# Attention shift and scale of layer 0: from two summed rows broadcast through DRAM to factors that TensorE makes for all 128 partitions

## The chip, the cores and the metric

The kernel runs on one core of a Trainium2 chip. The metric is the device time of one execution in microseconds (us); lower is better. The engines are PE (TensorE, matmuls; PEld is its weight load), DVE (VectorE), ACT (ScalarE), POOL (GpSimd) and SP, which here only issues DMAs. Each engine takes its own list of instructions in order and meets the others through semaphores.

## The reference

Two transformer blocks run one after the other on x of shape (2, 1024, 288), both conditioned on `cond` of shape (2, 288). Cut to what matters here:

```python
ada = silu(cond) @ W_ada + b_ada                  # (2, 6*288)
shift_msa, scale_msa, gate_msa, shift_mlp, scale_mlp, gate_mlp = split(ada, 6)
h = layernorm(x) * (1.0 + scale_msa) + shift_msa  # 288 numbers each for a batch element
x = x + gate_msa * attention(h, W_qkv, b_qkv, W_proj, b_proj)
h = layernorm(x) * (1.0 + scale_mlp) + shift_mlp
x = x + gate_mlp * (gelu(h @ W_fc1 + b_fc1) @ W_fc2 + b_fc2)
```

In layer 0 the attention goes over the 1024 tokens with 16 heads of 18; in layer 1 each token attends over its own heads.

## The kernel before

The 2048 tokens are 16 tiles of 128 tokens (tile t, eight for each of the two batch elements), with the 288 channels along the free dimension of `x_sb`. A modulation row therefore has to stand in all 128 partitions: `ada[:, b, place, :]` holds place 0 to 5 (shift, scale, gate of the attention; shift, scale, gate of the MLP) for batch element b.

At the entry of layer 0 the work is ordered by hand, as each engine's list.

- ACT's queue loads the first 576 columns of `W_ada` in three pieces of 96 rows (L1291) and `b_ada` for places 0 and 1 into 32 partitions each (L1293). ACT then makes silu of the condition, repeated 16 times so that it is 32 columns wide (`silu_t`, L1295).
- PE multiplies (`conditioning(0, 0, 6)`, L1743): three blocks of 96 rows by two places, each result 32 partitions high, both places in bank 6. The matrices are float32.
- DVE scales the bias (L952) and adds the product (L956, `ada_round`), which counts `ada_sum`. ACT stores the two rows in DRAM (L1300); SP waits for that (L558) and reads them back twice, broadcast to 128 partitions (`spread_ada`, issued at L531). Only behind that wait does SP issue the second half of x, the remaining columns of `W_ada` (L517), their biases (L521) and some small stores (L590).
- POOL waits for the product (`ada_mm`, L821), since `v_pad` lies over the loaded `W_ada`, fills `v_pad` (L823, L824), raises variances to the power -0.5 for tiles 0 to 7 (`first_rstd(0)`, L818), and then splits the qkv weights (`finish_weights`, L721 to L728), whose scaled form ACT makes (L1313 to L1320).
- DVE takes statistics of tiles 0 to 7 (L1217, L1223, L1225), prepares constants (L912 to L921), and goes through the tiles. `normalise` is two instructions, L934 (needs the scale row) and L938 (needs the shift row and `rstd`); `low_part` (L944) subtracts the float16 half that ACT copied (L1416). Four more statistics come in before tile 3 and before tile 4 (L1217).
- PE turns each tile (L1578, L1581), ACT copies it out (L1427), and after tiles 5, 8, 11 and 12 PE makes a projected part (L1685), which ACT takes (L1436), POOL splits (L747, L749) and DMAs copy into `stack_area` (L577, and L1541 on ACT's queue). Then the attention begins: for each score block PE makes a product (L1694) and DVE its row maximum (L964).

```python
            for t in range(NT + 1):
                first_statistics(STAT_AT.get(t, ()))
                if t - 1 == max(STAT_AT):
                    close_statistics(1)
                if t % TB == 0 and t < NT:
                    dve.wait_ge(msa_in[t // TB], 16)
                if t < NT:
                    normalise(0, t, t % 2, t, t, t // TB, 0)
```

Of the kernel before, what the change touches and what calls it, by code (L numbers as in the profile page):

```python
# [47 lines left out]
def hidden_blocks_kernel(nc, x, cond, qkv_w, qkv_b, proj_w, proj_b, fc1_w, fc1_b, fc2_w, fc2_b,  # L48
                         ada_w, ada_b, identity, ones_rows, lo_rows, max_rows, zeros, out):
    gelus = [ACT.Gelu_apprx_tanh, ACT.Gelu]  # L50
    with ExitStack() as ctx:
# [99 lines left out]
        def bank(i):  # L151
            return ps[:, i, :]
# [3 lines left out]
        def bank16(i, dt):  # L156
            return ps[:, i, :].bitcast(dt)

        def ada_columns(l, r, k):

            cols = slice(C * ADA_PLACES[r][0], C * (ADA_PLACES[r][-1] + 1))
            if (l, r) == (0, 1):
                area = (w_fc1, w_fc1, w_fc2)[k][:]
                area = area.rearrange("p k n -> p (k n)") if k < 2 else area.rearrange("p s f n -> p (s f n)")
                return area.bitcast(F32)[0:96, 4 * C * (k % 2):4 * C * (k % 2 + 1)]
            return ada_w_sb[l][:, k, cols]
# [17 lines left out]
        def ada_loads(l, r):  # L184

            return ada_in[r], 16 * (len(ADA_PLACES[r]) + 3) * (l + 1)

# [46 lines left out]
        ada_mm, ada_sum, ada_stored = sem("ada_mm"), sem("ada_sum"), sem("ada_stored")  # L234
        msa_in = [sem(f"msa_in{b}") for b in range(B)]
        late_in, gate_in = sem("late_in"), sem("gate_in")
        stat_raw, stat_agg, stat_ready, rstd_ready = (sem("stat_raw"), sem("stat_agg"), sem("stat_ready"),
# [220 lines left out]
        def freed(step):  # L458

            if step[0] == "S":  # L460
                return max_done, maximum_index(*step[1:]) + 1
            if step[0] == "P":
                return part_taken, QC * step[1] + step[2] + 1
            if step[0] == "M":
                return max_row, step[1] + 1
            if step[0] == "O":
                return o_ready, step[1] + 1
            if step[0] == "T":
                return hT_ready[0], step[1] + 1
            if step[0] == "V":  # L470
                return v_ready, step[1] + 1
            return ada_sum, 2

# [40 lines left out]
        def _(sp):  # L514
# [8 lines left out]
            def store_ada(l, r):  # L523

                sp.wait_ge(ada_sum, 2 * l + r + 1)
                for g, place in enumerate(ADA_PLACES[r]):
                    sp.dma_start(ada_rows[l, :, place, :], ada_cols[SW * g:SW * g + B, r, :]).then_inc(ada_stored, 16)
                sp.wait_ge(ada_stored, 16 * (6 * l + (6 if r else 2)))

# [27 lines left out]
            load_weights(0, 0, QKV_JOBS)  # L557
            sp.wait_ge(ada_stored, 16 * 2)  # L558
            for b in range(B):
                spread_ada(0, b, 0, 2, msa_in[b])  # L560
            load_tokens(2)
# [131 lines left out]
        def _(pool):  # L693
# [126 lines left out]

            pool.wait_ge(ada_mm, 1)  # L821
            flat = v_pad.rearrange("p t h d -> p (t h) d")
# [6 lines left out]
            for l in range(2):  # L829
                if l == 0:  # L830
                    split_part(0)
                    split_part(1)
                    split_maxima(0)
                    pool.wait_ge(ada_mm, 2)
                    for p in range(NPAIR):
# [55 lines left out]
                if l == 0:  # L891
                    with pool.Fori(1, 4) as t:
                        add_mlp(t)
                        invert(t - 1, stats + NT + t - 1)
                    pool.wait_ge(ada_mm, 4)
                    nc.gpsimd.memset(tokens[:, 0:8192], 0.0).then_inc(zeros_set, 1)
                    nc.gpsimd.memset(free4[:, 0:4096], 0.0).then_inc(zeros_set, 1)
                    nc.gpsimd.tensor_copy(v_rows, bias_row[:].unsqueeze(2).to_broadcast([P, H, P])
                                          ).then_inc(pads_set, 1)
# [9 lines left out]
        def _(dve):  # L909
# [37 lines left out]
            def ada_round(l, r, bk):  # L947

                rows = slice(0, SW * len(ADA_PLACES[r]))
                cols = ada_cols[rows, r, :]  # L950
                dve.wait_ge(*ada_loads(l, r))
                nc.vector.tensor_scalar(cols, cols, ada_plus[rows, r:r + 1], ada_factor[rows, r:r + 1], ALU.add, ALU.mult  # L952
                                        ).then_inc(ada_scaled, 1)
                dve.wait_ge(ada_scaled, 2 * l + r + 1)
                dve.wait_ge(ada_mm, 2 * l + r + 1)
                nc.vector.scalar_tensor_tensor(cols, bank(bk)[rows, 0:C], ada_factor[rows, r:r + 1], cols,  # L956
                                               ALU.mult, ALU.add).then_inc(ada_sum, 1)
# [16 lines left out]
            def normalise_o(p, bk):  # L974
# [4 lines left out]
                if p == 0:  # L979
                    dve.wait_ge(ada_stored, 16 * 6)  # L980
                nc.vector.reciprocal(recip.unsqueeze(3), o[:, :, :, D:D + 1]).then_inc(recip_done, 1)
# [98 lines left out]
            def mlp_chunk(l, c, last):  # L1080
                for f in range(FT):
# [9 lines left out]
                    if last and l == 0 and f % 2 == 0:  # L1091
                        i = f // 2
                        if i == 0:
                            for b in range(B):
                                dve.wait_ge(msa_in[b], 32)
                        if i:
# [136 lines left out]
            dve.wait_ge(ada_consts, 12)  # L1233
            ada_round(0, 0, 6)
            first_statistics(range(TB))
            close_statistics(0)
            constants()
            for l in range(2):
                if l == 0:
                    for t in range(NT + 1):  # L1240
                        first_statistics(STAT_AT.get(t, ()))
                        if t - 1 == max(STAT_AT):
                            close_statistics(1)
                        if t % TB == 0 and t < NT:
                            dve.wait_ge(msa_in[t // TB], 16)
                        if t < NT:
# [42 lines left out]
        def _(act):  # L1289
            for k in range(3):  # L1290
                nc.scalar.dma_start(*ada_weights(0, 0, k)).then_inc(ada_in[0], 16)  # L1291
            for g in range(len(ADA_PLACES[0])):
                nc.scalar.dma_start(*ada_bias(0, 0, g)).then_inc(ada_in[0], 16)  # L1293
            act.wait_ge(cond_in, 16 * B)
            nc.scalar.activation(silu_t[:].rearrange("p (k n b) -> p k n b", k=3, b=B), cond_t[:].rearrange(  # L1295
                "p (k b) -> p k b", b=B).unsqueeze(2).to_broadcast([96, 3, SW // B, B]), ACT.Silu).then_inc(silu_ready, 1)

            act.wait_ge(ada_sum, 1)
            for g, place in enumerate(ADA_PLACES[0]):
                nc.scalar.dma_start(ada_rows[0, :, place, :], ada_cols[SW * g:SW * g + B, 0, :]).then_inc(ada_stored, 16)  # L1300

# [116 lines left out]
            def take_v(t, bk):  # L1418
                if t == 0:
                    act.wait_ge(ada_mm, 1)  # L1420
                act.wait_ge(v_mm, t + 1)
# [145 lines left out]
        def _(pe):  # L1567
# [268 lines left out]
            def mlp_chunk(l, c, last):  # L1836
# [11 lines left out]
                if not last:  # L1848
                    if l == 0 and not isinstance(c, int):
                        pe.wait_ge(ada_sum, 4)  # L1850
                    for i in range(4):
# [33 lines left out]
            pe.wait_ge(silu_ready, 1)  # L1885
            conditioning(0, 0, 6)
            pe.wait_ge(const_ready, 1)
            for l in range(2):
                if l == 0:
                    for t in range(NT):  # L1890
                        turn(0, t % 2, t, t < 2)
                        for i, (n, at) in enumerate(PARTS_AT):
                            if t == at:
                                c = i % QC
                                pe.wait_ge(w_ready, QKV_JOBS)
                                pe.wait_ge(ada_sum, 1)
                                pe.wait_ge(hT_ready[0], TB // 2 * (c + 1))
# [76 lines left out]
```

## Time and profile before

| | us |
|---|---|
| median of 3 runs | 885.56 (883.44 to 885.78) |
| the profiled execution's own time | 885.84 |
| its span, first to last instruction | 883.8 |
| PE busy | 777.1 (88%) |
| DVE busy | 642.5 (73%) |
| ACT busy | 525.4 (59%) |
| POOL busy | 281.9 (32%) |

The profile is of one execution; times in it count from the span's start. A line such as L934 is a line of the kernel. In a timeline row stand start, duration, engine, line, operation, output and inputs, shape and count, and in brackets how long the engine sat idle before it and what ended that. The chain of waits follows the end of the execution back to what released each step. Neighbouring instructions of a like kind are merged into one row, and a float32 matmul is recorded as two.

### The profile page before, as it was taken

How to read it: one execution, taken by the hardware profiler on the slowest of the kernel's cores; microseconds unless marked ns; L12 is line 12 of the kernel's file. 1: busy time of each engine (PE TensorE's matmuls, PEld its weight loads, DVE VectorE, ACT ScalarE, POOL GpSimd, SP SyncE). 2: the span in 40 equal slices, each digit the busy share in tenths (PEclk: the TensorE clock that was granted, in tenths of full speed). 3: DMA queues.
4: the chain of work that ended last, by engine and by line, in shares of the span. 5: the costliest groups of instructions: out<-in, count | busy, mean ns of one | idle time of the engine just before them, and what ended most of it. 6: DMA issues, size and time to landing. Idle time of an engine off the chain costs nothing.

```text
span 883.8 us, 16502 instructions
## 1 busy us (share of the span) xinstructions
PE 777.1 (88%) x6096; PEld 361.9 (41%) x6096; DVE 642.5 (73%) x1277; ACT 525.4 (59%) x731; POOL 281.9 (32%) x369
## 2 busy tenths in 40 slices
PE   1578989899988989898898999999979986999996
PEld 0344222222222222222235466566646654566555
DVE  3879898988886898989827865656678897763531
ACT  4443676777775777767785724644547734734640
POOL 4320112214563422011014347241223565242122
PEclk9998999999999999999999999999999996999998
DMA  8312010111012110000030020102676620000000
GB/s 219 87 35 72 13 28 26 29 48 47 21 34 58 34 35 15 21 21 22 1 111 2 11 79 4 40 0 64 149 187 165 173 55 27 8 27 2 27 27 27
DMA packets 52128, 45.35 MB, mean 51 GB/s; under 512 B 23899, under 2 KB 41237, under 8 KB 52056
## 3 DMA queue, kind: packets, MB, share of 16 engines
q1 hardware_dynamic: 47613, 36.35, 16.0%
q10 hardware_dynamic: 4442, 8.04, 2.8%
q8 instruction: 45, 0.74, 0.4%
q14 instruction: 28, 0.22, 0.1%
HBM read 27.66 MB, written 9.46 MB: 42 GB/s over the span
## 4 chain that ended last, share of the span: by engine, by line
PE 53%; DVE 25%; ACT 5%; issue 4%; POOL 4%; DMA 4%; SPq 3%; ACTq 1%; DVEq 0%; POOLq 0%
PE ps L1866 12%; DVE row_max L964 12%; PE ps L1733 10%; PE ps L1694 8%; PE ps L1845 7%; PE ps L1721 3%; PE ps L1685 3%; PE ps L1632 3%; DVE mlp_area L1103 2%; SPq L577 2%; PE ps L1650 2%; DVE probs L938 1%; DVE probs L934 1%; ACT mlp_area L1497 1%; ACT mlp_area L1501 1%
## 5 line engine op out<-in xcount | busy, mean ns | idle before, releaser
L964 DVE TENSOR_REDUCE row_max<-ps 128x1 f32<-128x512 f32 x512 | 320.6, 683 | 50.2 <-PE ps L1694 49.3
L1456 ACT ACTIVATE probs<-ps 128x1024 f32<-128x1024 f32 x256 | 249.1, 1018 | 57.5 <-PE ps L1721 56.8
L1694 PE MATMUL ps<-stack_area 54*128 54x512 f16 x512 | 144.5, 390 | 28.1 <-DVE row_max L964 20.1
L1733 PE MATMUL ps<-probs,mlp_area 128*32 128x512 f32 x1024 | 137.1, 608 | 0.0
L1721 PE MATMUL ps<-stack_area 56*128 56x512 f16 x512 | 111.1, 386 | 7.2 <-ACT probs L1456 7.2
L1866 PE MATMUL ps<-w_fc,mlp_area 128*128 128x288 f16 x864 | 109.4, 289 | 4.7 <-DVE mlp_area L1103 4.7
L1694 PEld LDWEIGHTS ps<-stack_area 54*128 54x128 f16 x512 | 35.6, 93 | 186.0 <-DVE row_max L964 171.8
L1845 PE MATMUL ps<-mlp_area,w_fc 128*128 128x512 f16 x504 | 110.8, 379 | 0.8 <-ACT mlp_area L1497 0.8
L1497 ACT ACTIVATE mlp_area<-ps 128x512 f32<-128x512 f32 x72 | 42.9, 595 | 97.9 <-PE ps L1845 95.4
L1866 PEld LDWEIGHTS ps<-w_fc,mlp_area 128*128 128x128 f16 x864 | 84.6, 99 | 28.3 <-DVE mlp_area L1103 3.9
L767 POOL TENSOR_SCALAR neg_scaled<-neg_max 128x16 f32<-128x16 f32 x16 | 4.1, 254 | 271.9 <-DVE neg_max L971 271.9
L1845 PEld LDWEIGHTS ps<-mlp_area,w_fc 128*128 128x128 f16 x504 | 48.5, 98 | 60.7 <-ACT mlp_area L1497 4.3
L1116 DVE SCALAR_TENSOR_TENSOR probs<-ps,fc_bias 128x288 f32<-128x288 f32 x32 | 14.6, 457 | 78.1 <-PE ps L1866 78.1
L877 POOL TENSOR_TENSOR probs<-probs,ada (+2 forms) x32 | 26.1, 814 | 141.0 <-DVE probs L1116 140.7
L1103 DVE SCALAR_TENSOR_TENSOR mlp_area<-mlp_area 128x512 f16<-128x512 f32 x72 | 49.9, 701 | 17.7 <-ACT mlp_area L1501 17.5
L1501 ACT ACTIVATE mlp_area<-mlp_area 128x512 f16<-128x512 f32 x72 | 45.4, 630 | 2.7
L1721 PEld LDWEIGHTS ps<-stack_area 56*128 56x128 f16 x512 | 29.7, 94 | 36.5 <-ACT probs L1456 14.6
L938 DVE SCALAR_TENSOR_TENSOR probs<-probs,rstd,ada 128x288 f32<-128x288 f32 x64 | 37.0, 578 | 8.0 <-DVE probs L934 0.9
L1685 PE MATMUL ps<-tokens 128*126 128x512 f16 (+1 forms) x140 | 42.1, 428 | 0.4 <-ACT tokens L1427 0.4
L934 DVE SCALAR_TENSOR_TENSOR probs<-x_sb,mean_var,ada 128x288 f32<-128x288 f32 x64 | 36.1, 564 | 2.3 <-DMA ada<-ada_rows 1.4
L1632 PE MATMUL ps<-mlp_area,w_qkv 128*126 128x512 f16 (+1 forms) x147 | 34.7, 391 | 0.8 <-ACT mlp_area L1371 0.8
L1733 PEld LDWEIGHTS ps<-probs,mlp_area 128*32 128x32 f32 x1024 | 20.2, 108 | 36.8 <-issue 35.9
(170 smaller groups left out, 1070.5 us busy)
## 6 DMA issues: line engine op xcount, KB each, us to landing
stack_area<-tokens SPq DMA_DIRECT2D x124, 36.0 KB
qkv_rows<-part_area ACTq DMA_DIRECT2D x14, 252.0 KB
qkv_rows<-probs ACTq DMA_DIRECT2D x10, 252.0 KB
x_sb<-in_x SPq DMA_DIRECT2D x4, 576.0 KB, 7.3
w_raw<-in_L_cond_W_fc SPq DMA_DIRECT2D x4, 576.0 KB
tokens<-qkv_rows SPq DMA_DIRECT2D x64, 36.0 KB
v_sb<-qkv_rows SPq DMA_DIRECT2D x16, 144.0 KB
w_raw<-in_L_cond_fc_w SPq DMA_DIRECT2D x4, 576.0 KB
```

The costliest lines, as they stand in the source:

```text
L964: nc.vector.reduce_max(row_max[:, p % 2, t, j, half:half + 1], bank(bk), AX.X).then_inc(max_done, 1)
L1103: nc.vector.scalar_tensor_tensor(gs[:, f, 1, :], g_sb[f % 2], HS, gs[:, f, 0, :], ALU.mult, ALU.subtract).then_inc(g_split, 1)
L1456: nc.scalar.activation(probs[:, n % 2, 2 * c:2 * c + 2, :].rearrange("p h n -> p (h n)"), ps[:, 2 + 2 * c:4 + 2 * c, :].rearrange("p b n - ...
L1497: nc.scalar.activation(g_sb[f % 2], bank(2 + f % 2), gelus[l], scale=UN).then_inc(g_ready, 1)
L1501: nc.scalar.activation(gs[:, f, 0, :], g_sb[f % 2], ACT.Copy, scale=HS).then_inc(g_hi, 1)
L1632: mm = nc.tensor.matmul(bank(2 + n % 2)[0:end - first, :], w_qkv[:, w, first:end], piece_columns(i)[:, a, :], start=(x == 0), stop=(x == l ...
L1685: mm = nc.tensor.matmul(bank(bk)[0:rows], w_qk[:, w, row:row + rows], hT_all[:, a, t0:t0 + 512], start=(i == 0), stop=(i == len(PRODUCTS) ...
L1694: nc.tensor.matmul(bank(bk), stacks[rows, p % RING, 0, t * P:(t + 1) * P], stacks[rows, p % RING, 1, half * 512:(half + 1) * 512], start=T ...
L1721: mm = nc.tensor.matmul(bank(2 + 2 * c + j), stacks[rows, p % RING, 1, n * P:(n + 1) * P], stacks[rows, p % RING, 0, c * 512:(c + 1) * 512 ...
L1733: mm = nc.tensor.matmul(bank(6)[at:at + VW, :], v_pad[:, TB * (p // BPAIR) + n, 2 * (p % BPAIR) + j, :], probs[:, n % 2, 2 * c + j, :], st ...
L1845: mm = nc.tensor.matmul(bank(2 + f % 2), w_fc1[:, w, f * P:(f + 1) * P], h2T[:, a, :], start=(i == 0), stop=(i == len(PRODUCTS) - 1))
L1866: mm = nc.tensor.matmul(bank(4 + i % 2)[:, 0:C], gs[:, f, a, i * P:(i + 1) * P], w_fc2[:, w, f, :], start=(f == 0 and (a, w) == (0, 0)), s ...
```

## The change

For layer 0 and places 0 and 1 the condition is repeated 128 times instead of 32 (`silu_wide`), so that PE's product stands in all 128 partitions at once: 12 matmuls of 128 columns of weights by 288, for (b, place) in banks 6, 7, 4 and 5. The bias is broadcast by its load (L1293 goes), and DVE adds it (`msa_factors`): for b = 0 behind the first statistics, for b = 1 at tile 3 (`MSA_LATE`). The store in DRAM, the wait of SP's queue and the two broadcast reads of layer 0 go; the counts of the other rounds of `ada` are shifted by one. Layer 1 keeps its way.

```diff
+        MSA_LATE = 3
+        MSA_BANKS = ((6, 7), (4, 5))
+        silu_wide = part_area[0:96, 0:3 * B * P].rearrange("p (k b n) -> p k b n", k=3, b=B)
+        msa_bias_sb = ada[:, 0, 2:4, :]
...
             load_weights(0, 0, QKV_JOBS)
-            sp.wait_ge(ada_stored, 16 * 2)
-            for b in range(B):
-                spread_ada(0, b, 0, 2, msa_in[b])
             load_tokens(2)
...
-            pool.wait_ge(ada_mm, 1)
+            pool.wait_ge(msa_mm, 2 * B)
             flat = v_pad.rearrange("p t h d -> p (t h) d")
...
-            ada_round(0, 0, 6)
+
+            def msa_factors(b):
+
+                for g in range(2):
+                    dve.wait_ge(msa_mm, 2 * b + g + 1)
+                    nc.vector.scalar_tensor_tensor(ada[:, b, g, :], bank(MSA_BANKS[b][g])[:, 0:C], HS, msa_bias_sb[:, g, :],
+                                                   ALU.mult, ALU.add).then_inc(msa_sum, 1)
+
             first_statistics(range(TB))
             close_statistics(0)
+            dve.wait_ge(msa_bias_in, 16)
+            for g in range(2):
+                nc.vector.tensor_scalar(msa_bias_sb[:, g, :], msa_bias_sb[:, g, :], float(g), HS, ALU.add, ALU.mult
+                                        ).then_inc(msa_bias, 1)
+            dve.wait_ge(msa_bias, 2)
+            msa_factors(0)
             constants()
...
+                        if t == MSA_LATE:
+                            msa_factors(1)
                         if t % TB == 0 and t < NT:
-                            dve.wait_ge(msa_in[t // TB], 16)
+                            dve.wait_ge(msa_sum, 2 * (t // TB + 1))
...
-            for g in range(len(ADA_PLACES[0])):
-                nc.scalar.dma_start(*ada_bias(0, 0, g)).then_inc(ada_in[0], 16)
+            nc.scalar.dma_start(msa_bias_sb.rearrange("p s n -> p (s n)"), ada_b[0].rearrange("(a n) -> a n", a=1)[:, 0:2 * C]
+                                .to_broadcast([P, 2 * C])).then_inc(msa_bias_in, 16)
             act.wait_ge(cond_in, 16 * B)
+            nc.scalar.activation(silu_wide, cond_t[:].rearrange("p (k b) -> p k b", b=B).unsqueeze(3).to_broadcast(
+                [96, 3, B, P]), ACT.Silu).then_inc(silu_ready, 1)
...
-            act.wait_ge(ada_sum, 1)
-            for g, place in enumerate(ADA_PLACES[0]):
-                nc.scalar.dma_start(ada_rows[0, :, place, :], ada_cols[SW * g:SW * g + B, 0, :]).then_inc(ada_stored, 16)
...
             pe.wait_ge(silu_ready, 1)
-            conditioning(0, 0, 6)
+            pe.wait_ge(*ada_loads(0, 0))
+            for b in range(B):
+                for g in range(2):
+                    for k in range(3):
+                        mm = nc.tensor.matmul(bank(MSA_BANKS[b][g])[:, 0:C], silu_wide[:, k, b, :],
+                                              ada_columns(0, 0, k)[:, C * g:C * (g + 1)],
+                                              start=(k == 0), stop=(k == 2))
+                    mm.then_inc(msa_mm, 1)
+            pe.wait_ge(silu_ready, 2)
```

How DVE's list stands at the entry. Before, from the sum of the rows (L952, L956) to tile 0:

```order
L952 TENSOR_SCALAR v_sb<-v_sb,ada_plus,ada_factor 64x288 [waits ada_in0,ada_consts]
L956 SCALAR_TENSOR_TENSOR v_sb<-ps,ada_factor,v_sb 64x288 [waits ada_mm,ada_scaled]
L1217 BN_STATS v_sb<-x_sb 128x6 [waits x_in0]
...
L1225 TENSOR_SCALAR mean_var<-mean_var 128x8 [waits stat_agg]
L912 CAST ident<-ident 128x128 [waits const_in]
...
L934 SCALAR_TENSOR_TENSOR probs<-x_sb,mean_var,ada 128x288 [waits msa_in0]
L938 SCALAR_TENSOR_TENSOR probs<-probs,rstd,ada 128x288 [waits xn_done0,rstd_ready]
```

After the change, the same stretch and on to tile 3 (line numbers are those of the changed kernel; L1249 scales the bias, L1242 is `msa_factors`, L937 and L941 are `normalise`):

```order
L1220 BN_STATS v_sb<-x_sb 128x6 [waits x_in0,ada_consts]
...
L1249 TENSOR_SCALAR ada<-ada 128x288 [waits msa_bias_in]
L1249 TENSOR_SCALAR ada<-ada 128x288
L1242 SCALAR_TENSOR_TENSOR ada<-ps,ada 128x288 [waits msa_mm,msa_bias]
L1242 SCALAR_TENSOR_TENSOR ada<-ps,ada 128x288 [waits msa_mm]
L915 CAST ident<-ident 128x128 [waits const_in]
...
L937 SCALAR_TENSOR_TENSOR probs<-x_sb,mean_var,ada 128x288 [waits msa_sum]
L941 SCALAR_TENSOR_TENSOR probs<-probs,rstd,ada 128x288 [waits xn_done0,rstd_ready]
...
L1242 SCALAR_TENSOR_TENSOR ada<-ps,ada 128x288 [waits msa_mm] x2
L937 SCALAR_TENSOR_TENSOR probs<-x_sb,mean_var,ada 128x288
```

The statistics now stand ahead of all work on the modulation rows, and two additions stand between the statistics at tile 3 and tile 3 itself.

POOL's list keeps its order. At the entry it reads after the change:

```order
L815 MEMSET tokens 2x1024 [waits w_step]
L826 MEMSET mlp_area 128x256 [waits msa_mm,const_in]
L827 MEMSET mlp_area 128x256x13
L821 ISA
L821 TENSOR_TENSOR rstd<-mean_var,power 128x8 [waits stat_ready]
L724 TENSOR_TENSOR tokens<-w_raw,tokens 128x16x18 [waits w_scaled]
```

The first fill waits for the last of the 12 matmuls (`msa_mm`), where it waited for the last of 6 (`ada_mm`).

## Rows read from the trace of the kernel before

**Rows 1.** Busy time by stretch: us, then PE, PEld, DVE, ACT, POOL, PEclk, DMA share, GB/s
```profile
18.95:59.50 40.55, 22.43 (x185) 12.21 (x186) 31.87 (x69) 20.86 (x39) 16.88 (x18) 0.96 0.30 84
59.50:468.00 408.50, 372.46 (x2532) 108.35 (x2529) 337.97 (x579) 287.11 (x320) 103.79 (x144) 0.98 0.12 35
```

**Rows 2.** The chain of waits up to the attention: start us, us, what
```profile
2.74 6.38 DMA v_sb<-in_L_cond_b_ada
...
9.25 3.11 PE ps L1743 x12
...
13.53 1.13 DMA ada_rows<-v_sb
...
14.68 4.25 DMA ada<-ada_rows
...
59.51 18.62 DVE row_max L964 x31
```

**Rows 3.** DMAs issued from 2.1 to 2.3 us: KB each, median us to landing
```profile
x_sb<-in_x SPq DMA_DIRECT2D x2, 576.0 KB, 7.0
mlp_area<-in_L_cond_W_ada ACTq DMA_DIRECT2D x1, 216.0 KB, 5.6
```

**Rows 4.** Timeline of ACT, ACT's queue and PE around the product
```profile
1.68 0.48 ACTq L1291 DMA_DIRECT2D mlp_area<-in_L_cond_W_ada  x1
5.04 0.28 ACT L1295 ACTIVATE silu_t<-cond_t 96x96 f32<-96x96 f32 x1 [0.47 <-DMA cond_t<-in_cond]
9.71 0.21 PEld L1743 LDWEIGHTS ps<-mlp_area,silu_t 96*32 96x32 f32 x2 [0.27 <-issue]
10.19 0.21 PEld L1743 LDWEIGHTS ps<-mlp_area,silu_t 96*32 96x32 f32 x2 [0.27 <-issue]
54.49 1.63 PE L1743 MATMUL ps<-w_fc,silu_t 96*32 96x288 f32 x24
```

**Rows 5.** Timeline of PE, 35 to 52 us
```profile
36.09 3.25 PE L1685 MATMUL ps<-tokens 128*126 128x512 f16 x7
...
39.93 0.61 PE L1578 MATMUL ps<-ident,probs 128*128 128x128 f16 x4
...
41.28 0.38 PE L1578 MATMUL ps<-ident,probs 128*128 128x128 f16 x4 [0.55 <-ACT tokens L1427]
...
47.31 0.55 PE L1578 MATMUL ps<-ident,probs 128*128 128x128 f16 x4 [1.91 <-DVE probs L944]
...
50.94 0.39 PE L1578 MATMUL ps<-ident,probs 128*128 128x128 f16 x4
```

**Rows 6.** Timeline of POOL, 12 to 27 us
```profile
12.47 0.54 POOL L823 MEMSET mlp_area<- 128x256 f32 x1 [10.64 <-PE ps L1743]
12.86 3.15 POOL L824 MEMSET mlp_area<- 128x3328 f32 x1
16.96 1.66 POOL L818 TENSOR_TENSOR rstd<-mean_var,power 128x8 f32<-128x8 f32 x1 [0.95 <-DVE mean_var L1225]
18.59 1.60 POOL L721 TENSOR_TENSOR tokens<-w_raw,tokens 128x288 f16<-128x288 f32 x2
...
25.55 0.94 POOL L728 TENSOR_TENSOR w_qkv<-v_sb,w_mask 128x288 f16<-128x288 f32 x1
```

**Rows 7.** Timeline of DVE, 12 to 31 us
```profile
12.47 0.51 DVE L956 SCALAR_TENSOR_TENSOR v_sb<-ps,ada_factor,v_sb 64x288 f32<-64x288 f32 x1 [2.82 <-PE ps L1743]
12.90 2.96 DVE L1217 BATCH_NORM_STATS2 v_sb<-x_sb 128x6 f32<-128x288 f32 x8
...
18.95 0.68 DVE L934 SCALAR_TENSOR_TENSOR probs<-x_sb,mean_var,ada 128x288 f32<-128x288 f32 x1 [1.38 <-DMA ada<-ada_rows]
19.73 0.78 DVE L938 SCALAR_TENSOR_TENSOR probs<-probs,rstd,ada 128x288 f32<-128x288 f32 x1
20.43 0.98 DVE L934 SCALAR_TENSOR_TENSOR probs<-x_sb,mean_var,ada 128x288 f32<-128x288 f32 x1
...
25.82 1.52 DVE L1217 BATCH_NORM_STATS2 v_sb<-x_sb 128x6 f32<-128x288 f32 x4
```

More of the change, by code:

```diff
@@ L184, in ada_loads @@
         def ada_loads(l, r):
-            return ada_in[r], 16 * (len(ADA_PLACES[r]) + 3) * (l + 1)
+            return ada_in[r], 16 * ((len(ADA_PLACES[r]) + 3) * (l + 1) - (0 if r else len(ADA_PLACES[0])))
         FIRST_BANKS = (4, 5, 6, 7)
@@ L235, in hidden_blocks_kernel @@
         msa_in = [sem(f"msa_in{b}") for b in range(B)]
+        msa_bias_in, msa_bias, msa_mm, msa_sum = sem("msa_bias_in"), sem("msa_bias"), sem("msa_mm"), sem("msa_sum")
         late_in, gate_in = sem("late_in"), sem("gate_in")
@@ L471, in freed @@
                 return v_ready, step[1] + 1
-            return ada_sum, 2
+            return ada_sum, 1
         def stack_copy(p, x, j, i):
@@ L523, in store_ada @@
             def store_ada(l, r):
-                sp.wait_ge(ada_sum, 2 * l + r + 1)
+                sp.wait_ge(ada_sum, 2 * l + r)
                 for g, place in enumerate(ADA_PLACES[r]):
                     sp.dma_start(ada_rows[l, :, place, :], ada_cols[SW * g:SW * g + B, r, :]).then_inc(ada_stored, 16)
-                sp.wait_ge(ada_stored, 16 * (6 * l + (6 if r else 2)))
+                sp.wait_ge(ada_stored, 16 * (6 * l + (4 if r else 0)))
             def spread_ada(l, b, first, end, done):
@@ L833, in _ @@
                     split_maxima(0)
-                    pool.wait_ge(ada_mm, 2)
+                    pool.wait_ge(ada_mm, 1)
                     for p in range(NPAIR):
@@ L894, in _ @@
                         invert(t - 1, stats + NT + t - 1)
-                    pool.wait_ge(ada_mm, 4)
+                    pool.wait_ge(ada_mm, 3)
                     nc.gpsimd.memset(tokens[:, 0:8192], 0.0).then_inc(zeros_set, 1)
@@ L953, in ada_round @@
                                         ).then_inc(ada_scaled, 1)
-                dve.wait_ge(ada_scaled, 2 * l + r + 1)
-                dve.wait_ge(ada_mm, 2 * l + r + 1)
+                dve.wait_ge(ada_scaled, 2 * l + r)
+                dve.wait_ge(ada_mm, 2 * l + r)
                 nc.vector.scalar_tensor_tensor(cols, bank(bk)[rows, 0:C], ada_factor[rows, r:r + 1], cols,
@@ L979, in normalise_o @@
                 if p == 0:
-                    dve.wait_ge(ada_stored, 16 * 6)
+                    dve.wait_ge(ada_stored, 16 * 4)
                 nc.vector.reciprocal(recip.unsqueeze(3), o[:, :, :, D:D + 1]).then_inc(recip_done, 1)
@@ L1094, in mlp_chunk @@
                             for b in range(B):
-                                dve.wait_ge(msa_in[b], 32)
+                                dve.wait_ge(msa_in[b], 16)
                         if i:
@@ L1419, in take_v @@
                 if t == 0:
-                    act.wait_ge(ada_mm, 1)
+                    act.wait_ge(msa_mm, 2 * B)
                 act.wait_ge(v_mm, t + 1)
@@ L1849, in mlp_chunk @@
                     if l == 0 and not isinstance(c, int):
-                        pe.wait_ge(ada_sum, 4)
+                        pe.wait_ge(ada_sum, 3)
                     for i in range(4):
@@ L1895, in _ @@
                                 pe.wait_ge(w_ready, QKV_JOBS)
-                                pe.wait_ge(ada_sum, 1)
+                                pe.wait_ge(msa_sum, 2 * B)
                                 pe.wait_ge(hT_ready[0], TB // 2 * (c + 1))
```

## The prediction

> **What bounds the kernel now.** I read the page first: no engine is full, so what an edit is worth depends on its stage. The windows view then cuts the span at 59.5 us. In the attention behind it PE and DVE are busy for 372 and 338 of 408.5 us; in the entry, from 18.95 to 59.5 us, PE is busy for 22.4 of 40.55 and DVE for 31.9 [rows 1]. The change touches only the entry, so I ask when the attention starts, and take any shift of that start to pass through whole: the work behind it waits for engines, and no row of the attention waits for one of the loads that move.
>
> The chain of waits says what sets that start [rows 2]. The reader is to see four links: the bias load lands at 9.12 us, PE's product runs to 12.36, the sum goes out to DRAM at 13.5 and comes back at 18.93, and only then does DVE start tile 0. The edit cuts exactly this loop. From 18.95 us DVE carries the chain nearly alone, until the row maxima begin at 59.5.
>
> Before believing the gain I asked what else tile 0 waits for. It is two instructions [rows 7]: L934 at 18.95 needs the broadcast row, L938 at 19.73 needs `rstd` from POOL. POOL's timeline [rows 6] shows `rstd` made from 16.96 to 18.62 us, behind two fills that could start only at 12.47, when PE had finished with the weights they overwrite. So `rstd` was just 1.1 us ahead of its user. That second gate stays, and the change moves it.
>
> **The product on PE.** Before, 6 float32 matmuls (12 records) took 3.10 us: the two places are each 32 columns wide and ran side by side, and a step of two records took 0.48 us (9.71 to 10.19) [rows 4]. So 12 records were 6 steps. The other row of this kind agrees: 24 records, four abreast, are also 6 steps, and took 1.63 us at 54.49 [rows 4]. Less about 0.2 us until the last result is out (my estimate from both rows), a step costs 0.48 us in the first and 0.24 us in the second. The ratio is two because the clock is at the lower level (1.2 GHz) in one and at the upper (2.4) in the other.
>
> After the change there are 12 matmuls (24 records) that are 128 columns wide. Nothing runs beside them, so they are 24 steps: 24 x 0.48 + 0.2 = 11.7 us at the lower level, 24 x 0.24 + 0.2 = 6.0 us at the upper.
>
> They start earlier. The last piece of `W_ada` is issued at 1.68 us and takes 5.6 [rows 3, 4], so it lands at 7.28 and PE starts at about 7.4 instead of 9.25. The wider silu is no gate: the old one starts at 5.04 us and takes 0.28 for 96 columns [rows 4]; even eight times that ends at 7.3.
>
> Which level? After idling, PE ran its 7 matmuls at 36.09 us in 3.25 us, and its transposes were still at 0.61 us for four at 39.93, but at 0.38 at 41.28. Another burst began at 47.31 with 0.55 and was at 0.39 by 50.94 [rows 5]. [...] I take 4.4: 9.2 steps at 0.48, the other 14.8 at 0.24 (3.6 us), 0.2 to drain, 8.2 us in all. PE ends at 15.6 us, where it ended at 12.36. Bounds: 13.4 if at the upper level throughout, 19.1 if it never rises.
>
> **POOL behind it.** The fills begin 0.11 us after PE's end and finish 3.54 us later (12.47 to 16.01) [rows 6]: 19.25. `rstd` then takes 1.66 to 1.7 with about 0.1 to start it: 21.0. L938 of tile 0 starts 0.1 later, at 21.1 instead of 19.73: **+1.4 us**. By PE's bounds it is -0.8 to +4.9.
>
> **DVE before tile 0.** The old round goes (it stood in idle time). The statistics need the first two loads of x, issued by 2.3 us and 7.0 on the way [rows 3], so they can run from about 9.3 to 12.3 us instead of 12.90 to 15.86 [rows 7]. Aggregation and constants took DVE from there to 17.57, where its idle 1.38 us before L934 began [rows 7]: 1.7 us. Scaling the bias twice and adding twice is four instructions, which I price at 0.51 each like the addition of before (L956): 2.0. The first L934 could go at about 16.0. None of this counts: L938 waits for POOL until 21.1. The cover is over 4 us.
>
> **Two additions at tile 3.** `msa_factors(1)` puts two instructions on DVE's busy stretch, which is the chain. The nearest row is the same operation on 64 partitions, also with its product in PSUM, at 0.51 us [rows 7]; time on DVE goes by elements in a partition. The other bound is 0.98, an L934 beside POOL's splitting of weights [rows 7]. That splitting lasts 7.9 us (18.59 to 26.49) [rows 6] and begins as `rstd` ends, so it ends 7.8 us behind L938 of tile 0. The additions come 7.6 us behind it (25.82 + 1.52 - 19.73, the statistics before tile 3) [rows 7], with next to nothing of it left. I take 2 x 0.51 = **+1.0 us**, up to 2.0.
> The Trainium skill (SBUF — State Buffer, Who interferes with whom) says that a DVE instruction with one input in SBUF, outside the two-port modes, doesn't contend with GpSimd; these have one. By it the term is 1.0 however long POOL works, by the row of L934 2.0; no row of this trace shows such an instruction beside POOL's splitting.
>
> **POOL's splitting stands later against DVE.** Before, it had begun 1.1 us ahead of L938; now they begin together. The seven slow instructions that follow are slow in both kernels, and the statistics at 25.82 are not slowed (1.52 us for four, as 2.96 for eight [rows 7]). I take **+0.2 us**, at most 0.5.
>
> **Loads and queues.** On SP's queue the wait and two reads of 288 KB go; x's second half, the rest of `W_ada`, its biases and the small stores are issued some 7 us earlier, right behind the weight loads. Their first user is the statistics at 25.82, so being early buys nothing and costs nothing. ACT's queue carries one load of 288 KB instead of two of 36 KB; its user comes at about 13 us. ACT can scale the weights as soon as they are there, for it no longer waits for the sum; POOL reads them only from 21.0, where it did from 18.59. Cover in each case: over 2 us.
>
> **Sum:** 1.4 + 1.0 + 0.2 = +2.6 us on the profiled execution's 885.84 us (span 883.8 and 2.0 around it), **888.4 us**. That execution is 0.3 above the median of 885.56. About 0.3% (2.7 us) is what a measurement of this kernel can tell from no change, so this forecast lies at that border: 888.2 is where slower begins.
>
> **The rivals.**
> - *The clock stays low through the whole product.* For it: the burst at the start comes from a long idle PE, and before, all 12 records ran at the lower level. Against: both later bursts rose within 5.2 us. It gives +4.9 + 1.0 + 0.2 = +6.1, 891.9 us.
> - *PE is at the upper level soon.* PE ends at 13.4 us, `rstd` at 18.9, L938 at 18.9 to 19.0: -0.8 + 1.2 = +0.4, 886.2 us. Against it: the burst at 9.25 was at the lower level.
> - *The second gate isn't one, and the loop's removal is paid out* (the other side). If POOL has `rstd` by about 16.6, DVE alone decides: L934 at 16.0, L938 at 16.7, so -3.0 + 1.2 = -1.8, 884.0 us, and 882.5 if x lands 1.5 us earlier. That needs PE to end by 11.1 us, with steps of 0.15 us; nothing in [rows 4] comes near. For it speaks only that POOL's spans are rough. The Trainium skill (DMA: Bandwidth & Descriptors, Anatomy of one DMA) gives each DMA about 2 us of fixed cost, which alone would promise 4 us for the two in series; here the loop took 5.9 us from the sum to L934 [rows 2, 7], but it is not what ends last any more.
> - *Later bursts fall otherwise.* The 7 matmuls at 36.09 us stand in the chain at the lower level [rows 2, 5] and DVE idles behind them. With all shifted, one such burst may meet the upper level, which halves its 3.25 us, or lose it. I price it at -1.5 or +1.5 on top of +2.6: 886.9 or 889.9.
> - *The change doesn't do what it says:* excluded by the listing of instructions; the broadcast reads are gone.
>
> **How the numbers follow.** Forecast with its own range of 887.4 to 889.4: 0.60, split by the 888.2 border into 0.34 slower and 0.26 no change. Clock low throughout: 0.13, slower. Upper level soon: 0.08, no change. Gate gone: 0.06, nearly all faster by chance of what more it brings, 0.05 and 0.01. Later bursts: 0.13, of which 0.06 slower, 0.05 no change, 0.02 faster. Sum: slower 0.53, same 0.40, faster 0.07. The range for 8 in 10 reaches from the upper-level case (886.2, less the spread of the runs) to the low-clock case: 885.6 to 892.0.
>
> **What would show it.** After: PE's 24 records from about 7.4 to 15.6 us, their step falling from 0.48 to 0.24 on the way; POOL's fills from 15.7; `rstd` ending near 21; DVE idle for over 4 us before its first L938 (L941 of the changed kernel), ended by POOL; two additions of 0.5 us before tile 3; the first row maxima some 2.6 us later than 59.5. Wrong if L941 first runs before 19.7 us, if DVE's idle before it is ended by anything but POOL, or if the row maxima start later by another amount than the tiles do.

## The result and the profile after

The changed kernel takes 888.73 us (median of 20 runs, 884.28 to 893.59); the kernel before, run beside it, 885.42 us (median of 20, 879.54 to 889.91). The ratio is 1.0037 with a 95% interval of 1.0021 to 1.0053: 3.3 us slower, just over the border that the prediction named. Two further comparisons (below) gave 1.0028 and 1.0021, that is 3.0 and 1.8 us; the three together average 2.7 us. The profiled execution took 885.21 us with a span of 882.8, at the low end of its own runs: one profile of each kernel would even show the change as 0.6 us faster. So the profile is read here for what moved, and the runs for how much it is worth.

The page of the changed kernel, its engines and the group that the prediction watched (L938 of before is L941 here):

```profile
PE 782.0 (89%) x6108; PEld 366.6 (42%) x6108; DVE 643.1 (73%) x1281; ACT 525.8 (60%) x732; POOL 281.3 (32%) x369
...
L941 DVE SCALAR_TENSOR_TENSOR probs<-probs,rstd,ada 128x288 f32<-128x288 f32 x64 | 37.2, 581 | 13.2 <-POOL rstd L821 5.8
```

The reader is to see the last column: DVE idled 5.8 us ahead of L941 for `rstd`. The chain of waits of the changed kernel shows the same link in order of time (start us, us, what), and answers to [rows 2]:

```profile
1.69 6.44 DMA mlp_area<-in_L_cond_W_ada
...
8.26 7.89 PE ps L1906 x24
...
16.65 3.10 POOL mlp_area L827
...
19.83 1.69 POOL rstd L821
...
21.54 0.96 DVE probs L941
...
29.32 0.72 DVE ada L1242 x2
...
38.88 3.18 PE ps L1701 x7
...
61.91 18.63 DVE row_max L967 x31
```

The store and the broadcast that stood in [rows 2] are gone. In their place stand PE's product for 7.9 us where it took 3.1, POOL's fill and `rstd`, and further on two additions. The long group of row maxima, by which the prediction dated the attention, starts at 61.91 us where it started at 59.51, +2.40 (both times from the chain). The timeline of the changed kernel, with the same places as [rows 4, 6, 7]:

```profile
4.69 0.84 ACT L1313 ACTIVATE part_area<-cond_t 96x768 f32<-96x768 f32 x1 [0.66 <-DMA cond_t<-in_cond]
...
8.26 7.87 PE L1906 MATMUL ps<-mlp_area,part_area 96*128 96x288 f32 x24 [8.26 <-DMA mlp_area<-in_L_cond_W_ada]
...
15.27 0.51 DVE L937 SCALAR_TENSOR_TENSOR probs<-x_sb,mean_var,ada 128x288 f32<-128x288 f32 x1
...
16.26 0.54 POOL L826 MEMSET mlp_area<- 128x256 f32 x1 [14.43 <-PE ps L1906]
...
19.83 1.68 POOL L821 TENSOR_TENSOR rstd<-mean_var,power 128x8 f32<-128x8 f32 x1
...
21.54 0.96 DVE L941 SCALAR_TENSOR_TENSOR probs<-probs,rstd,ada 128x288 f32<-128x288 f32 x1 [5.76 <-POOL rstd L821]
...
24.21 0.97 DVE L947 TENSOR_TENSOR probs<-probs 128x288 f16<-128x288 f32 x1
...
27.80 1.53 DVE L1220 BATCH_NORM_STATS2 v_sb<-x_sb 128x6 f32<-128x288 f32 x4
...
28.43 0.72 POOL L731 TENSOR_TENSOR w_qkv<-v_sb,w_mask 128x288 f16<-128x288 f32 x1
...
29.25 0.80 DVE L1242 SCALAR_TENSOR_TENSOR ada<-ps,ada 128x288 f32<-128x288 f32 x2
29.97 0.50 DVE L937 SCALAR_TENSOR_TENSOR probs<-x_sb,mean_var,ada 128x288 f32<-128x288 f32 x1
```

L937 of tile 0 starts at 15.27 us; as L934 of the kernel before it waited for the broadcast until 18.95. So the loop's removal did what it says, 3.7 us early. L941 right behind it then waits for POOL, and starts 1.8 us later than L938 did.

### The profile page after: what moved, and what is told of

The parts are those of the page before. It is cut to its first block, busy times and chain, and to the rows that moved or that the text cites. A ratio compares the mean times of both kernels' runs of the same rounds, so it can differ in the third digit from the quotient of the medians.

```text
span 882.8 us, 16526 instructions
## 1 busy us (share of the span) xinstructions
PE 782.0 (89%) x6108; PEld 366.6 (42%) x6108; DVE 643.1 (73%) x1281; ACT 525.8 (60%) x732; POOL 281.3 (32%) x369
## 3 DMA queue, kind: packets, MB, share of 16 engines
q10 hardware_dynamic: 4482, 8.26, 2.9%
## 4 chain that ended last, share of the span: by engine, by line
PE 57%; DVE 26%; ACT 5%; issue 4%; POOL 4%; DMA 2%; SPq 1%; DVEq 0%; ACTq 0%; POOLq 0%
DVE row_max L967 12%; PE ps L1882 12%; PE ps L1749 11%; PE ps L1710 8%; PE ps L1861 7%; PE ps L1701 4%; PE ps L1648 4%; PE ps L1737 3%; DVE mlp_area L1106 2%; DVE probs L941 2%; DVE probs L937 2%; PE ps L1617 1%; ACT mlp_area L1513 1%; ACT mlp_area L1517 1%; ACT probs L1472 1%
## 5 line engine op out<-in xcount | busy, mean ns | idle before, releaser
L941 DVE SCALAR_TENSOR_TENSOR probs<-probs,rstd,ada 128x288 f32<-128x288 f32 x64 | 37.2, 581 | 13.2 <-POOL rstd L821 5.8
L937 DVE SCALAR_TENSOR_TENSOR probs<-x_sb,mean_var,ada 128x288 f32<-128x288 f32 x64 | 35.9, 562 | 1.0 <-issue 0.8
```

What stands on the lines that cost most here:

```text
L941: nc.vector.scalar_tensor_tensor(hn[u], xn[u], rstd[:, bass.ds(t, 1)], ada[:, b, s, :], ALU.mult, ALU.add).then_inc(h_ready[ph], 1)
```

## The experiments

Theory A is the prediction's: the gate is POOL (the fills wait for the whole of PE's product, `rstd` stands behind them), and two additions stand on DVE's chain. The rivals: B, the loads that are now issued earlier slow the first transfers; C, the clock level at the product; D, moving `rstd` is a gain that the kernel before could have had as well. Three groups of runs were made, each on one chip beside the kernel before (medians of before 884.91, 885.42 and 885.23 us). "Distance" is from the first L938 or L941 to the start of `neg_max`, the first instruction behind the first block of row maxima.

**The change again.** No edit, in the first and third group.

> The changed kernel itself, as the yardstick for the kernels beside it. Theory (the gate moved from the broadcast to POOL's rstd): 1.003 to 1.004 of before, first L941 near 21.5 us, ended by POOL, row maxima from 61.9 us. Rival (the 0.37% came from elsewhere, as in the other stages): the start of the row maxima would not be later than before's 59.5 us.

> The changed kernel once more, as the yardstick on this chip: 1.003 to 1.004 of before.

Measured: 887.86 us, ratio 1.0028 [1.0005, 1.0051] (in brackets the 95% interval, here and below), and 886.98 us, 1.0021 [0.9996, 1.0047], an interval that just takes in no change. L941 starts at 21.66 and 20.88 us, the product at 8.18 and 7.43. What follows: the change costs 2 to 3 us, and the gate of one and the same kernel moves by 0.8 us with the arrival of its weights.

**`rstd` ahead of the fills**, in the changed kernel and, alone, in the kernel before (there the wait is `ada_mm, 1`):

```diff
+            first_rstd(0)
             pool.wait_ge(msa_mm, 2 * B)
...
-            first_rstd(0)
             for i in range(QKV_JOBS):
```

> POOL makes rstd of tiles 0 to 7 ahead of its wait for the product and of the two fills. Theory (POOL's gate): rstd ends near 15 us, the first L941 starts within 0.2 us of the end of the first L937, about 15.9 us instead of 21.5. The copies on ACT stand behind its scaling of the weights, which ended at 20.05 us, so low_part of tile 0 starts at about 20.6 instead of 24.2: a gain of 3.6 us on the changed kernel, at most 5.6. That is about the time of before, or a little under it (0.998 to 1.001 of before). Rival (the added work of PE or DVE itself costs the time, not the gate): no change against the changed kernel, 1.003 to 1.004 of before.

> The kernel before, with rstd of tiles 0 to 7 made ahead of POOL's wait for the product and of the fills. Theory (before, the broadcast row ended last, and rstd was 1.1 us ahead of its user): rstd can't come ahead of the statistics, which end at 16.8 us; the fills and the splitting of weights move a little; no change, 0.998 to 1.002 of before, first L938 still ended by the chain through the broadcast read. Rival (moving rstd gains by itself, whatever the change does): the 3 us that the same edit gave on the changed kernel would show here too, 0.9966.

Measured: 886.0 us, 0.9996 [0.9978, 1.0015] in the changed kernel; 885.55 us, 1.0007 [0.9991, 1.0023] in the one before. The timeline of the first (changed kernel, `rstd` first):

```profile
12.80 1.77 POOL L821 TENSOR_TENSOR rstd<-mean_var,power 128x8 f32<-128x8 f32 x1 [10.97 <-DVE mean_var L1228]
...
15.21 0.52 DVE L941 SCALAR_TENSOR_TENSOR probs<-probs,rstd,ada 128x288 f32<-128x288 f32 x1
...
19.03 1.01 ACT L1336 ACTIVATE w_mask<-w_mask,lo_row 128x864 f16<-128x864 f16 x1
...
20.07 0.78 ACT L1432 ACTIVATE probs<-probs 128x288 f16<-128x288 f32 x2
...
20.55 0.71 DVE L947 TENSOR_TENSOR probs<-probs 128x288 f16<-128x288 f32 x1 [3.77 <-ACT probs L1432]
```

The gate opens at once: L941 goes from 21.54 to 15.21 us. But of 6.3 us only 3.7 arrive at L947 (24.21 to 20.55), for ACT is still scaling the weights of the layer, a row of work that starts when the weights land at 12.3 us and ends at 20.04. A third gate stands right behind the second. In the time it is 1.9 us against the change itself in the same group; those two intervals overlap, while the change's own of 20 runs (1.0021 to 1.0053) lies wholly above this one. In this profile the row maxima start 4.2 us earlier than in the change (57.70 for 61.90), but their first block ends only 3.0 us earlier: behind the first ones, 14 matmuls of L1692 take 3.37 us instead of 1.89, and DVE waits for them. In the kernel before the same edit moved L938 by 0.14 us only:

```profile
17.46 1.66 POOL L818 TENSOR_TENSOR rstd<-mean_var,power 128x8 f32<-128x8 f32 x1 [15.63 <-DVE mean_var L1225]
...
18.97 0.52 DVE L934 SCALAR_TENSOR_TENSOR probs<-x_sb,mean_var,ada 128x288 f32<-128x288 f32 x1 [0.93 <-DMA ada<-ada_rows]
19.59 0.52 DVE L938 SCALAR_TENSOR_TENSOR probs<-probs,rstd,ada 128x288 f32<-128x288 f32 x1
...
22.54 0.46 DVE L944 TENSOR_TENSOR probs<-probs 128x288 f16<-128x288 f32 x1 [1.38 <-ACT probs L1416]
```

There L934 still waits for the broadcast, and L944 behind it then waits for ACT, whose scaling of the weights starts only when it has stored the sum (14.34 us) and ends at 22.03. So D falls: `rstd` first is a gain only where the loop is gone.

**PE's product longer.** The half of the second condition is computed twice over, with the same result:

```diff
-                    for k in range(3):
+                    for k in (0, 1, 2, 0, 1, 2) if b else range(3):
```

> The changed kernel with the product of the second batch element computed twice (6 matmuls, 12 records more; the same result). No user of the first batch element waits for them; only POOL's wait and the additions at tile 3 do. Theory (PE's end, POOL's fills and rstd are one chain to L941): 12 records at the upper clock level are 12 x 0.24 = 2.9 us, so L941 starts 2.9 us later than in the changed kernel, near 24.4 us, and the row maxima too: 1.0065 to 1.007 of before. Rival (the added work is hidden): 1.003 to 1.004.

Measured: 891.93 us, 1.0074 [1.0051, 1.0097]. The chain of waits of this kernel:

```profile
8.63 11.88 PE ps L1906 x36
...
21.01 3.08 POOL mlp_area L827
...
24.18 1.68 POOL rstd L821
...
25.89 0.96 DVE probs L941
```

The product ends 4.36 us later than in the change (20.51 for 16.15) and L941 starts 4.35 later, at 25.89 us. The expectation said 24.4: it priced the 12 added records at 2.9 us, the upper level, and the product grew by 4.0 (11.88 for 7.89). The time lies 3.6 us above sp_wait (below), which has the change's order and stood in the same group, and the two intervals just touch (1.0051). From PE's end to L941 it is 5.4 us in every kernel of this order (5.39 in the change, 5.38 here, 5.41 and 5.39 in the two runs below with products of 9.12 and 9.16 us). So L941 follows PE's end, as A says, and in rstd_first, where the chain from PE's end through POOL to L941 is cut, it doesn't.

**The loads back to their old time.**

```diff
             load_weights(0, 0, QKV_JOBS)
+            sp.wait_ge(msa_sum, 2)
             load_tokens(2)
```

> The changed kernel, but SP's queue waits for the first batch element's additions (about 14.6 us) before it issues the second half of x and the rest of W_ada, as it did before. Theory (these loads are needed only from 27.8 us on, and don't touch the product): no change against the changed kernel, 1.002 to 1.004 of before, PE's start at 7.6 to 8.3 us as in its other runs. Rival (the earlier loads crowd the entry and are what costs): back to the time of before.

Measured: 888.36 us, 1.0029 [1.0007, 1.0051], as slow as the change. Its x loads were issued at 14.44 us, where the change had them at 8.47, and nothing came back. B falls for what stands on SP's queue.

**The bias load behind the silus on ACT's queue** (the broadcast read of 288 KB moved from L1310 to behind L1315).

> ACT issues the broadcast load of the bias (288 KB) behind its two silus instead of ahead of them. Theory (the wider bias load shares the way with the last piece of W_ada, which took 6.4 us to land instead of 5.6): PE starts at about 7.4 us instead of 8.26 and all behind it 0.8 us earlier. Rival (the landing scatters by itself): PE starts at 8.2 us again, and nothing changes. The bias comes later, by about 14 us, which still lies ahead of POOL's 21.5.

Measured: 888.48 us, 1.0042 [1.0015, 1.007]. The last piece of `W_ada` took 5.9 us on the way where the change had 6.4, but without this edit the same piece took 5.6 in again2 and 6.8 in twice. No gain in time; whether the wider load slows the weights stays open.

**The additions in DVE's idle time** (`msa_factors(1)` right behind `constants()` and not at tile 3).

> The two additions for the second batch element stand behind the constants, where DVE idles for POOL, and not at tile 3. Theory (they lie on the chain at tile 3): they took 0.72 us of the chain and now cost nothing: 0.7 us less than the changed kernel, row maxima from about 61.2 us. Rival (DVE has slack by tile 3): the row maxima start at 61.9 us as in the changed kernel.

Measured: 889.87 us, 1.0046 [1.0028, 1.0063]. The timeline of this kernel at tile 3:

```profile
28.74 1.52 DVE L1220 BATCH_NORM_STATS2 v_sb<-x_sb 128x6 f32<-128x288 f32 x4
30.19 0.49 DVE L937 SCALAR_TENSOR_TENSOR probs<-x_sb,mean_var,ada 128x288 f32<-128x288 f32 x1
```

Statistics to L937 is 1.45 us where the change took 2.17 (27.80 to 29.97): 0.72 us saved there, to the letter what the chain lists for L1242. The time doesn't show it: the median (of 7 runs) is 2.0 us above the change's in the same group, and the intervals overlap. In its profile the product took 9.43 us (7.87 in the change), which moves L941 to 22.48; the row maxima still start slightly earlier than in the change (61.77 for 61.90 us), but their first block ends 1.1 us later, since 14 matmuls of L1691 (L1692 of the change) take 3.45 us there instead of 1.89. A gain of 0.7 is smaller than what PE's two levels do from one execution to the next. On the time of this edit alone the run is inconclusive.

**PE kept busy ahead of the product**, with 13 unused matmuls of 2 rows (work that the kernel doesn't need, 128 columns by 512, started as soon as `tokens` is filled with ones).

> The changed kernel with 13 matmuls of 2 rows by 128 by 512 columns (float16, results unused) on PE from about 1.9 us until the product starts. Theory (the product is a chain link, and runs half of its time at the lower clock level): if PE is at the upper level when the product starts, its 24 records take about 6.0 us instead of 7.9 to 9.4 and all behind it comes 2 to 3 us earlier, 1.000 to 1.001 of before. If these matmuls use too little of the array to raise the clock, 1.003 to 1.004 as the changed kernel. Rival (POOL, not PE, sets the start): no change with a product of 6 us.

Measured: 889.02 us, 1.0048 [1.0028, 1.0068]. The timeline and, under it, the windows of the product's instructions in this kernel (stretch, length, PE busy, PEld busy, PEclk, DMA share, GB/s):

```profile
1.89 5.72 PE L1904 MATMUL ps<-tokens 2*128 2x512 f16 x13 [1.89 <-POOL tokens L816]
...
8.08 9.12 PE L1910 MATMUL ps<-mlp_area,part_area 96*128 96x288 f32 x24 [0.47 <-DMA mlp_area<-in_L_cond_W_ada]
```

```profile
8.00:12.00 4.00, 3.92 (x8) 2.86 (x9) 1.00 0.92 331
12.00:16.00 4.00, 4.00 (x13) 3.00 (x12) 1.00 1.06 246
```

Eight records in 3.92 us are 0.49 each, the lower level, 0.47 us after 5.7 us of matmuls. The edit didn't raise the clock (why is open), so it didn't test C. C keeps its part otherwise: over the eleven profiles with 24 records, the change's own among them, the product took 7.9 to 8.1 us in six and 9.0 to 9.4 in five.

**Both places early, and the weights' splitting ahead of the fills.** Three builds on `rstd` first: `MSA_LATE = 1` as well (late1); the splitting of the weights ahead of the fills on top (fills_late); with it the weights spread over the tiles on ACT, `WEIGHTS_AT` (all_three). The diff shows the edits of all_three.

```diff
-        MSA_LATE = 3
+        MSA_LATE = 1
...
-        WEIGHTS_AT = {-1: (0, 1, 2)}
+        WEIGHTS_AT = {-1: (0,), 0: (1,), 2: (2,)}
...
+            first_rstd(0)
+            for i in range(QKV_JOBS):
+                finish_weights(i)
             pool.wait_ge(msa_mm, 2 * B)
...
-            first_rstd(0)
-            for i in range(QKV_JOBS):
-                finish_weights(i)
```

> The kernel rstd_first, and the second batch element's additions not at tile 3 but ahead of tile 1, where DVE idled 3.8 us for ACT. Theory (they are on the chain at tile 3 and free in that idle time): 0.7 us less than rstd_first, 0.998 to 1.000 of before; from the first low_part (20.55 us) to tile 3 it takes 0.72 us less. Rival (bursts of PE at the lower clock level decide more than 0.7 us): no difference that can be measured.

> As late1, with POOL's two fills of v_pad behind the splitting of the weights. Theory: the splitting then runs from about 14.7 us, while DVE idles for ACT, but stays bound to ACT's scaling, which ends at 20.05 us, so its last third still lies beside DVE's tiles 1 and 2: about 1 us fewer of slowed DVE instructions, 0.997 to 0.999 of before. Rival (the splitting doesn't slow DVE): no change against late1.

> As fills_late, with ACT's scaling of the three weight blocks spread: one ahead of tile 0, one behind tile 0, one behind tile 2. Theory (ACT's scaling is the gate once rstd is early): low_part of tile 0 starts at about 16.5 us instead of 20.55, and 2 to 3 us of the 4 stay: 0.993 to 0.996 of before. Rival (PE's part after tile 5 then waits for the last block's split, or the loads of the second half of x arrive too late for the statistics at tile 3): no better than fills_late.

Measured: 884.77 us, 0.9987 [0.9971, 1.0002]; 883.29 us, 0.9978 [0.9963, 0.9993]; 884.14 us, 0.9979 [0.9962, 0.9996]. The second and third beat the kernel before, by 1.9 and 1.1 us, and the change in the same group by 3.7 and 2.8; late1's interval takes in no change. late1 and fills_late are 1.5 us apart with overlapping intervals, so what the order of the fills gives by itself is not settled. late1's own stretch came as expected: from the first `low_part` to tile 3 it took 4.81 us where rstd_first took 5.49. The timeline of fills_late:

```profile
8.62 8.95 PE L1906 MATMUL ps<-mlp_area,part_area 96*128 96x288 f32 x24 [8.62 <-DMA mlp_area<-in_L_cond_W_ada]
...
13.21 1.77 POOL L821 TENSOR_TENSOR rstd<-mean_var,power 128x8 f32<-128x8 f32 x1 [11.38 <-DVE mean_var L1228]
...
15.07 0.68 DVE L915 CAST ident<-ident 128x128 f16<-128x128 f32 x1
...
16.97 1.05 DVE L937 SCALAR_TENSOR_TENSOR probs<-x_sb,mean_var,ada 128x288 f32<-128x288 f32 x1
...
18.57 0.94 POOL L726 TENSOR_TENSOR w_qkv<-v_sb,w_qkv 128x288 f16<-128x288 f32 x1
18.84 0.81 DVE L1242 SCALAR_TENSOR_TENSOR ada<-ps,ada 128x288 f32<-128x288 f32 x2
...
20.90 0.98 DVE L947 TENSOR_TENSOR probs<-probs 128x288 f16<-128x288 f32 x1
...
22.41 0.54 POOL L829 MEMSET mlp_area<- 128x256 f32 x1
```

POOL waits for PE no longer; the fills run last, where nobody waits for them, though this product is one of the long ones. The additions stand where DVE of rstd_first idled for ACT. The long group of row maxima starts at 57.03 us (59.51 before, 61.91 in the change). all_three missed its expectation (0.993 to 0.996) and bore out its rival. ACT reaches its conversions sooner, but DVE then works on the additions and tile 1, so L947 runs at 19.76 us (20.90 in fills_late, 16.5 expected); the last weights come later, and with them POOL's fills. These now meet DVE's small step behind the statistics:

```profile
28.14 3.15 POOL L830 MEMSET mlp_area<- 128x3328 f32 x1
...
29.14 2.17 DVE L1228 TENSOR_SCALAR mean_var<-mean_var 128x8 f32<-128x8 f32 x1
```

L1228 takes 0.17 us in fills_late and in the change. Here it takes 2.17, ends with the fill, and stands in the chain with all of it: 2.0 us lost, more than the 0.6 by which the maxima start later than in fills_late (57.61). That the fill holds it up is read from the two rows, not tested.

## Why the prediction was right, step by step

It said 888.4 us, +2.6 on the profiled execution; the runs say 888.73 and +3.3 on the medians, inside the narrow range as well. Its likeliest case is the one that happened, and rstd_first and twice, which open and lengthen the gate, show that its cause was the right one.

- *PE's start*, 7.4 us: 8.26 here, 6.73 to 8.63 in the other profiles of kernels with the wide product. The last piece of `W_ada` took 6.4 us, not 5.6. The silu was no gate (5.5).
- *The product*, 8.2 us with its step falling on the way: 7.87, and the windows of the changed kernel's L1906 show the fall (same columns as above). The 4.4 us at the lower level that the sum uses is shown by no run: of the two bursts it leans on, the second was at the upper level by 50.94 us, 3.6 us after its start, which bounds the moment from above only. By the prediction's own prices for a step, 7.87 us is 8 of 24 steps at the lower level and 9.43 us, the longest, 14 to 15 (my estimate); the sum took 9.2. That PE ended so near the forecast in this profile is in part luck: it started 0.9 us later than foreseen and ran 0.3 us shorter.

```profile
8.00:10.00 2.00, 1.74 (x4) 1.34 (x5) 1.00 0.98 300
10.00:12.00 2.00, 2.00 (x6) 1.43 (x5) 1.00 1.00 388
12.00:14.00 2.00, 2.00 (x9) 1.56 (x9) 1.00 1.05 237
```

- *The gate*, L941 at 21.1 us, +1.4: 21.54, +1.8. The part behind PE was foreseen as 5.5 us and is 5.4; what was under-sized is when PE ends (16.15 for 15.6). Over the seven runs with the order of the change L941 starts at 21.8 us on average (20.88 to 22.61), so the term is +2.1 rather than +1.4. This is the mis-sized term of the sum.
- *Two additions*, 1.0 us: 0.72 in the chain and 0.72 by factors_idle. The price was taken from one instruction alone (0.51); two in a row read 0.80 for both, and 0.72 of that is in the chain. With POOL's splitting beside them (18.84 us in fills_late, L726 running) they read 0.81: no slower, so the bound of 2.0 was not needed. The Trainium skill (SBUF — State Buffer, Who interferes with whom) says that a DVE instruction with at most one input in SBUF, outside the two-port modes, doesn't contend with GpSimd, and these rows agree; L937, with two, takes 1.05 instead of 0.51 in the same stretch.
- *The splitting against DVE*, +0.2: from L938 or L941 of tile 0 to the statistics it is 6.09 us before and 6.26 after, +0.17.
- *Loads and queues*, nothing: sp_wait bears it out. *DVE idle over 4 us before L941, ended by POOL*: 5.76.
- *Row maxima 2.6 us later*: 2.40 in this profile. With 2.1 in place of 1.4, 0.7 of 1.0 and 0.2, the terms make +3.0; the gate was priced too low and the additions too high, and the two errors partly cancel.

Of the rivals, "the gate isn't one" needed PE to end by 11.1 us; it ended at 16.15. (The fixed 2 us that this rival takes from the Trainium skill, DMA: Bandwidth & Descriptors, Anatomy of one DMA, is stated in that section for DMAs issued by GpSimd; ACT and SP issued these two, and they took 1.13 and 4.25 us in the chain of [rows 2].) "The clock stays low throughout" came a part of the way in five of eleven profiles (9.0 to 9.4 us for the product, never 11.7). "Upper level soon" was never seen. "Later bursts fall otherwise" was right in kind and far too small: it was priced at 1.5 us, and the profiles show 4. The distance is 59.0 us in the change and 58.4 in the kernel before (the additions and the splitting add 0.9; 0.3 of it is gone again by the row maxima), but 63.1 to 63.5 in twice, warm and sp_wait. PE's timeline of the changed kernel, and then of twice:

```profile
44.93 1.70 PE L1701 MATMUL ps<-tokens 128*126 128x512 f16 x7 [0.37 <-ACT tokens L1443]
...
57.38 1.63 PE L1759 MATMUL ps<-w_fc,silu_t 96*32 96x288 f32 x24
```

```profile
49.27 3.06 PE L1701 MATMUL ps<-tokens 128*126 128x512 f16 x7
...
62.48 3.10 PE L1759 MATMUL ps<-w_fc,silu_t 96*32 96x288 f32 x24
```

The same 7 and 24 records take 1.4 and 1.5 us longer at the lower level, and DVE waits behind them. late1's profile has both as well (3.05 and 3.10 us). That this loss belongs to the profiled execution, and not to every execution of the edited kernel, can be read from the times on record. These four profiled executions took 896.92 (twice), 893.48 (warm), 893.03 (sp_wait) and 889.53 us (late1), each 4.5 to 5.0 us above the median of its own kernel; the ten other profiled executions, where these 24 records (L1759, or L1743 of before) take 1.63 us, lie between 3.5 below theirs and 0.8 above. What decides it from one execution to the next, and whether an edit makes it more frequent, stays open.

One thing the profiles can't decide lies behind the attention. At 584.50 us of before the change is 1.6 us late (586.12), yet its last group of fc2 matmuls starts 0.97 earlier (861.67 for 862.64). The chain of before has a store at 626 us and a load of 7.0 us at 638, where the chain of this execution has matmuls, and then a store at 643. Only repeated runs tell which is typical.

## What to carry to other kernels

Before a wait is cut, list what else its waiter needs and when each is ready: here the next instruction of the same tile needed a result that was only 1.1 us ahead, and it hung on an engine whose own release the change made 3.8 us later. A buffer that is filled again as soon as a product has read it ties its filler to that product. Whatever doesn't need the product goes ahead of the fill, and then the next gate (here ACT's scaling) sets what is gained. A fill that is moved also has new neighbours, as L1228 of all_three shows. Where a gain is under 1 us and PE works in bursts, a pair of profiles misleads in both directions: compare medians of many runs, and check how far the profiled execution lies from its own kernel's median.

## What the runs showed of the hardware

The granted clock in a stretch can read full while the durations are those of the lower level: 1.00 in all windows of the product above, with 8 records in 3.92 us in one and 13 in 4.00 in the next. The mean over the execution differs too, 0.977 before and 0.963 after, and most of that is the stretch from 20 to 40 us. Before, and then in the change:

```profile
20.00:40.00 20.00, 8.82 (x64) 4.86 (x65) 18.12 (x44) 9.23 (x17) 8.27 (x9) 1.00 0.48 135
```

```profile
20.00:40.00 20.00, 6.09 (x51) 3.46 (x52) 17.52 (x43) 7.04 (x15) 10.93 (x11) 0.50 0.25 60
```

Yet four transposes take 0.61 us and the first 7 matmuls of a part 3.25 us in both, so the lower reading isn't what makes the change slower. In stretches this short the durations tell the level, not that column. The moment at which the product's step falls isn't fixed to its start: with nearly equal starts (7.76 and 7.64 us) it took 7.88 us in bias_late and 9.43 in factors_idle. In warm, 5.7 us of matmuls with 2 rows ended 0.47 us ahead of the product, and its first eight records still took 0.49 us each.

Beside POOL's work some small DVE instructions grow far more than others: the cast L915 takes 0.22 us in the change and 0.68 in fills_late beside the splitting, and L1228 takes 0.17 and, in all_three beside a fill, 2.17.
